# One transformer layer on one core: windowed attention whose contexts come out turned the other way, with a shorter selection and new orders of work

## The reference, cut to what matters

```python
h = concat([tokens(x), txt], axis=1)                 # (16, 165, 256): 1 + 36 + 128 tokens
h = h + attn(layernorm(h))
h = h + ffn(layernorm(h))                            # quantised matmuls, depthwise conv, silu

def attn(x):                                         # 16 query heads, 4 key heads, head size 16
    xq, xk = rope(x @ Wq), rope(x @ Wk)
    xv = x @ Wv
    keys, values = repeat(xk, 4), repeat(xv, 4)
    scores = einsum('bqhd,bkhd->bhqk', xq, keys) / 4
    mask = abs(idx[:, None] - idx[None, :]) <= 32    # a band of 65 keys
    attn = softmax(where(mask, scores, -inf))
    ctx = einsum('bhqk,bkhd->bqhd', attn, values).reshape(b, s, 256)
    return ctx @ Wo
```

## Time and profile before

| | |
|---|---|
| median of 3 runs | 399.84 us |
| the runs | 399.84, 400.05, 396.22 us |
| the profiled execution | 396.99 us |
| its span, first to last instruction | 395.2 us |
| mean granted TensorE clock | 0.987 of 2.4 GHz |
| PE busy | 364.5 us, 92% of the span |
| DVE, ACT, POOL busy | 301.8, 256.5, 215.0 us |

### The profile page before, as it was taken

How to read it: one execution, slowest core, us unless ns; L and a number is a source line. 1 busy time by engine, 2 the same in 40 slices (tenths; PEclk the granted TensorE clock), 3 DMA queues, 4 the chain that set the end, 5 groups by cost and what they waited for, 6 DMA issues and landing times.

```text
span 395.2 us, 8402 instructions
## 1 busy us (share of the span) xinstructions
PE 364.5 (92%) x3033; PEld 273.6 (69%) x3037; DVE 301.8 (76%) x639; ACT 256.5 (65%) x483; POOL 215.0 (54%) x245
## 2 busy tenths in 40 slices
PE   6799799999999999999989999999999988987886
PEld 2376557777877886678767876788678866853743
DVE  2246649654599879888998698959895998799795
ACT  3213436568786779677868686769767966672552
POOL 5406589688479928892689427971994006001000
PEclk9889989999999999999999999999999999999999
DMA  7671521201000012002000220022011100000101
GB/s 235 166 181 41 153 99 29 54 13 28 20 19 2 2 48 50 22 21 53 19 0 2 57 48 2 2 61 44 11 27 44 27 2 13 25 2 0 35 2 35
DMA packets 21907, 16.71 MB, mean 42 GB/s; under 512 B 12435, under 2 KB 20936, under 8 KB 21865
## 3 DMA queue, kind: packets, MB, share of 16 engines
q1 hardware_dynamic: 20970, 15.11, 15.3%
q10 hardware_dynamic: 895, 1.06, 1.0%
HBM read 9.82 MB, written 3.38 MB: 33 GB/s over the span
## 4 chain that ended last, share of the span: by engine, by line
PE 65%; DVE 17%; ACT 7%; issue 5%; DMA 4%; POOL 1%; SPq 1%; DVEq 0%; ACTq 0%; POOLq 0%
PE bank L1784 8%; PE bank L1864 8%; PE bank L1835 7%; PE bank L1878 6%; PE bank L1937 5%; PE bank L1938 4%; PE bank L1907 4%; DMA shared<-in_x 4%; PE bank L1855 3%; PE bank L1731 3%; PE bank L1981 3%; DVE shared L1635 2%; PE bank L1898 2%; PE bank L1797 2%; PE bank L1847 2%
## 5 line engine op out<-in xcount | busy, mean ns | idle before, releaser
L1501 DVE TENSOR_REDUCE mx<-bank 120x4 fp32r<-120x376 f32 (+3 forms) x88 | 44.1, 506 | 26.8 <-PE bank L1847 26.2
L1273 ACT COPY pT<-bank 94x480 f32<-94x480 f32 (+3 forms) x88 | 48.1, 554 | 21.7 <-PE bank L1864 21.3
L1265 ACT ACTIVATE pr<-bank 120x376 f32<-120x376 f32 (+3 forms) x88 | 39.6, 453 | 27.1 <-PE bank L1855 26.2
L1864 PE MATMUL bank<-cst,pr 120*94 120x120 f32 (+3 forms) x352 | 51.3, 270 | 2.6 <-ACT pr L1265 2.5
L1835 PE MATMUL bank<-kbd,q_hl 128*120 128x376 f32 (+3 forms) x176 | 51.1, 374 | 1.6 <-issue 0.9
L1113 POOL TENSOR_TENSOR rs<-ve,half_neg 110x3 f32<-110x3 f32 x16 | 16.7, 1044 | 62.8 <-DVE ve L1529 47.2
L1937 PE MATMUL bank<-xT_hi,w1T 128*128 128x330 f32 x128 | 44.2, 351 | 1.3 <-DVE late L1584 0.9
L1864 PEld LDWEIGHTS bank<-cst,pr 120*94 120x94 f32 (+3 forms) x352 | 36.1, 122 | 10.0 <-ACT pr L1265 6.0
L1120 POOL TENSOR_SCALAR xn<-h,mv,rs 110x256 f32<-110x256 f32 x21 | 27.6, 1321 | 25.3 <-PE bank L1772 24.9
L1135 POOL TENSOR_TENSOR rc<-qk,cst 110x320 f32<-110x320 f32 x22 | 20.0, 908 | 38.9 <-ACT qk L1236 37.9
L1938 PE MATMUL bank<-xT_lo,w1T 128*128 128x330 f32 x128 | 39.5, 314 | 0.0
(11 more groups left out here) (131 smaller groups left out, 877.7 us busy)
## 6 DMA issues: line engine op xcount, KB each, us to landing
kbd<-shared SPq DMA_DIRECT2D x56, 41.2 KB, 2.1
out<-h SPq DMA_DIRECT2D x7, 330.0 KB
wn<-in_w SPq DMA_DIRECT2D x2, 1024.0 KB, 6.6
shared<-in_x SPq DMA_DIRECT2D x4, 432.0 KB
h<-in_txt SPq DMA_DIRECT2D x1, 770.0 KB
late<-in_lin SPq DMA_DIRECT2D x1, 768.0 KB, 7.6
vw<-v_rows SPq DMA_DIRECT2D x8, 94.0 KB
v_rows<-qk SPq DMA_DIRECT2D x8, 82.5 KB
```

The source lines that it names most:

```text
L1265: nc.scalar.activation(pr[:, g % 3, 0:HKV * WIDTH[j]], S_BANKS[g % 2][0:QP, 0:HKV * WIDTH[j]], ACT.Exp, scale=HD ** -0.5).then_inc(exped, 1)
L1273: nc.scalar.copy(pT[0:WIDTH[j], g % 3, :], S_BANKS[g % 2][0:WIDTH[j], 0:HKV * QP]).then_inc(p_kept, 1)
L1501: nc.vector.tensor_reduce(mx[:, g % 4, :].bitcast(F32R), S_BANKS[g % 2][0:QP, 0:HKV * WIDTH[j]].rearrange("p (k c) -> p k c", k=HKV), axis ...
L1864: o = nc.tensor.transpose(S_BANKS[g % 2][0:w, kv * QP:(kv + 1) * QP], pr[:, g % 3, kv * w:(kv + 1) * w], ident[0:QP, 0:QP])
```

## The change: what it does

The operands of `context` change places. `pT` (the turned probabilities, 120 columns) is now the stationary operand and `vw` the moving one, cut to 17 columns (16 values and the ones; `VS` goes from 32 to 17). All four `kv` use the whole array instead of a strip each, and the result has queries on the partitions. So `keep_ctx` and `turn_ctx` are gone, `norm` reads `C_BANK` itself, and the bank is free for the next group when `norm` is done rather than when the copy is. `select` is one fp32 transpose for every two windows (48 in all), after which the two windows of a transpose lie in the lower and upper half of the partitions; `keep_sel` puts heads and windows in place with four copies of 64 partitions instead of one. The clearing of `vw` on POOL is left out. The four `keep_clock` products that stood behind the last `turn_ctx` stand behind the last `context`. All orders of work (the tables) are new.

```diff
-VS = 2 * HD
+VS = HD + 1
...
-                nc.scalar.copy(ctxP[:, :, js[0] * QB:(js[-1] + 1) * QB],
-                               N_BANK[:, 0:len(js) * QP // 2].rearrange("p (q c) -> p c q", c=2)).then_inc(sel_kept, 1)
+                at = js[0] * QB
+                turned = N_BANK[:, 0:(len(js) + 1) // 2 * QP].rearrange("p (i q c e) -> p e c i q", q=QB, c=2, e=2)
+                for odd in range(2):
+                    cnt = (len(js) + 1 - odd) // 2
+                    for e in range(2):
+                        dst = ctxP[QK * e:QK * (e + 1), :, at:at + len(js) * QB].rearrange("p c (j q) -> p c j q", q=QB)
+                        o = nc.scalar.copy(dst[:, :, odd::2, :], turned[QK * odd:QK * (odd + 1), e, :, 0:cnt, :])
+                o.then_inc(sel_kept, 1)
...
             def norm(n, k):
                 cnt = len(GROUPS[k])
-                dve.wait_ge(ctx_turned, NG * n + k + 1)
-                src = N_BANK[0:QP, 0:cnt * 128].rearrange("p (c v) -> p c v", v=VS)
+                dve.wait_ge(ctx_done, NB * n + GROUPS[k][-1] + 1)
+                if n or k:
+                    dve.wait_ge(ctx_picked, NG * n + k)
+                src = C_BANK[0:QP, 0:cnt * HKV * VS].rearrange("p (c v) -> p c v", v=VS)
...
                 if j % SLOTS == 0 and (n or k):
-                    pe.wait_ge(ctx_kept, NG * n + k)
-                col = (j % SLOTS) * QP
+                    pe.wait_ge(ctx_normed, NG * n + k)
                 for kv in range(HKV):
-                    o = nc.tensor.matmul(C_BANK[VS * kv:VS * (kv + 1), col:col + QP], vw[n % 2][0:WIDTH[j], j, :, kv],
-                                         pT[0:WIDTH[j], g % 3, kv * QP:(kv + 1) * QP], start=True, stop=True)
+                    at = (j % SLOTS * HKV + kv) * VS
+                    o = nc.tensor.matmul(C_BANK[0:QP, at:at + VS], pT[0:WIDTH[j], g % 3, kv * QP:(kv + 1) * QP],
+                                         vw[n % 2][0:WIDTH[j], j, :, kv], start=True, stop=True)
                 o.then_inc(ctx_done, 1)
...
             def select(n, k):
...
-                half = QP // 2
-                for c in range(len(GROUPS[k])):
-                    for e in range(2):
-                        o = nc.tensor.matmul(N_BANK[QK * e:QK * (e + 1), c * half:(c + 1) * half], ctxn[:, c, :],
-                                             ident[0:QP, e:QP:2], start=True, stop=True)
+                cnt = len(GROUPS[k])
+                for c in range(0, cnt, 2):
+                    src = ctxn[:, c:min(c + 2, cnt), :].rearrange("p c v -> p (c v)")
+                    o = nc.tensor.transpose(N_BANK[0:QK * min(2, cnt - c), c // 2 * QP:(c // 2 + 1) * QP], src,
+                                            ident[0:QP, 0:QP])
                 o.then_inc(ctx_picked, 1)
...
 ONCE = {
-    'pe.patches': (3, 4, 11, 12),
+    'pe.patches': (2, 10, 11, 17),
```

More of the change, by code:

```diff
@@ L143 @@
     'pe.turn_xn': (
[L144 to L151, removed]
+        (3, 4),
+        (18, 21),
+        (67, 70),
+        (129, 139),
+        (208, 213),
+        (284, 290),
+        (356, 361),
+        (428, 433),
     ),
     'pe.project': (
[L154 to L159, removed]
@@ L160 @@
-        (383, 388, 399),
-        (461, 464, 475),
+        (6, 7, 9),
+        (26, 29, 36),
+        (76, 78, 97),
+        (151, 154, 167),
+        (223, 231, 241),
+        (298, 303, 308),
+        (365, 371, 379),
+        (448, 451, 456),
     ),
     'pe.turn_q': (
[L164 to L171, removed]
+        (12, 13, 15),
@@ L172 @@
+        (45, 50, 59),
+        (101, 111, 120),
+        (178, 186, 194),
+        (247, 256, 268),
+        (318, 335, 340),
+        (386, 391, 403),
+        (474, 477, 489),
     ),
     'pe.turn_k': (
[L174 to L181, removed]
+        (14, 16),
+        (62, 65),
+        (123, 126),
+        (200, 204),
+        (273, 277),
+        (343, 346),
+        (406, 417),
@@ L242 @@
+        (112, 147, 160),
+        (182, 209, 234),
+        (259, 283, 309),
+        (332, 376, 385),
+        (411, 432, 457),
+        (479, 509, 526),
+        (546, 569, 584),
     ),
     'pe.out_proj': (
[L244 to L251, removed]
+        (55, 85, 92),
+        (116, 155, 164),
+        (188, 217, 238),
+        (270, 306, 312),
@@ L252 @@
+        (342, 382, 389),
+        (420, 454, 460),
+        (496, 522, 529),
+        (557, 581, 585),
     ),
     'pe.turn_xs': (
[L254 to L261, removed]
+        (128,),
+        (199,),
+        (272,),
+        (347,),
+        (421,),
+        (493,),
+        (560,),
+        (590,),
     ),
     'pe.up': (
[8 rows of a table removed]
[8 rows of a table added]
     ),
     'pe.turn_max': (
-        (176,),
-        (253,),
-        (329,),
@@ L277 @@
[L277 to L281, removed]
+        (173,),
+        (246,),
+        (319,),
+        (395,),
+        (468,),
+        (538,),
+        (586,),
+        (600,),
     ),
     'pe.spread': (
[L284 to L291, removed]
+        (179,),
+        (249,),
+        (323,),
+        (400,),
+        (472,),
+        (542,),
+        (587,),
@@ L292 @@
+        (601,),
     ),
     'pe.down': (
[L294 to L301, removed]
+        (189, 191, 195),
+        (262, 263, 266),
+        (336, 337, 338),
+        (412, 413, 414),
+        (483, 484, 488),
+        (551, 552, 555),
+        (588, 589, 591),
+        (602, 602, 602),
     ),
     'dve.stats1': (
-        (5,),
@@ L305 @@
-        (9,),
+        (4,),
+        (10,),
         (13,),
-        (17,),
+        (18,),
         (37,),
-        (101,),
-        (149,),
+        (97,),
+        (146,),
         (198,),
@@ L343 @@
     'dve.max_s': (
[8 rows of a table removed]
[8 rows of a table added]
     ),
     'dve.norm': (
[L354 to L361, removed]
+        (23, 30, 40),
+        (48, 56, 67),
+        (91, 104, 127),
+        (142, 154, 175),
+        (190, 203, 227),
+        (238, 251, 272),
+        (285, 306, 321),
+        (334, 346, 366),
     ),
     'dve.add_att': (
[L364 to L371, removed]
+        (31, 41, 44),
+        (53, 79, 84),
+        (98, 126, 134),
+        (150, 178, 183),
+        (199, 228, 233),
+        (247, 275, 280),
+        (298, 322, 328),
+        (344, 367, 370),
     ),
@@ L532 @@
+        (123, 131, 133),
+        (172, 179, 184),
+        (225, 231, 233),
+        (270, 273, 278),
+        (326, 336, 337),
     ),
     'act.keep_k': (
-        (16, None),
-        (46, 49),
-        (89, 93),
-        (144, 148),
-        (198, 201),
-        (250, 257),
-        (307, 311),
-        (358, 362),
+        (17, None),
+        (45, 47),
+        (85, 86),
+        (137, 139),
+        (188, 189),
+        (236, 239),
+        (284, 288),
+        (339, 346),
     ),
     'act.exp': (
[8 rows of a table removed]
[8 rows of a table added]
@@ L582 @@
+        (77, 102, 114),
+        (126, 147, 165),
+        (182, 204, 217),
+        (232, 264, 269),
+        (285, 310, 319),
+        (333, 359, 365),
+        (378, 389, 402),
     ),
     'act.quant_x': (
-        (83,),
-        (135,),
-        (188,),
-        (243,),
-        (297,),
-        (351,),
-        (401,),
+        (78,),
+        (129,),
+        (180,),
+        (230,),
+        (283,),
+        (332,),
+        (377,),
         (),
@@ L716 @@
         (10,),
-        (12,),
-        (16,),
+        (13,),
+        (15,),
         (19,),
-        (22,),
+        (20,),
         (25,),
@@ L1349, in _ @@
             work = {name: due("act." + name) for name in (
-                "exp", "keep_xn", "keep_qk", "keep_q", "keep_ctx", "keep_sel", "quant_x", "high_x", "mid", "keep_p", "keep_k", "tanh", "abs_g", "conv_g", "keep_w", "sort_a", "keep_pix_a", "keep_patch")}
+                "exp", "keep_xn", "keep_qk", "keep_q", "keep_sel", "quant_x", "high_x", "mid", "keep_p", "keep_k", "tanh", "abs_g", "conv_g", "keep_w", "sort_a", "keep_pix_a", "keep_patch")}
             for q in TICKS:
@@ L1359, in _ @@
                     keep_q(n, t)
-                for n, k in work["keep_ctx"].get(q, ()):
-                    keep_ctx(n, k)
                 for n, k in work["keep_sel"].get(q, ()):
@@ L1985, in _ @@
             work = {name: due("pe." + name) for name in (
-                "shift", "context", "scores", "turn_p", "turn_xn", "project", "turn_q", "turn_k", "turn_ctx", "select", "out_proj", "turn_xs", "up", "turn_max", "spread", "down", "turn_pix", "patches", "sum_w", "turn_w")}
+                "shift", "context", "scores", "turn_p", "turn_xn", "project", "turn_q", "turn_k", "select", "out_proj", "turn_xs", "up", "turn_max", "spread", "down", "turn_pix", "patches", "sum_w", "turn_w")}
             for q in TICKS:
@@ L2003, in _ @@
                     turn_k(n, part)
-                for n, k in work["turn_ctx"].get(q, ()):
-                    turn_ctx(n, k)
                 for n, k in work["select"].get(q, ()):
```

322 lines of the change are left out of this document (134 added, 188 removed), and 176 rows, old and new, of the table ORDER.

## The result

| | before | changed |
|---|---|---|
| median | 398.5 us (396.22 to 400.05, 4 runs) | 409.56 us (408.43 to 410.15, 4 runs) |
| ratio, 95% interval | | 1.0286 (1.0236 to 1.0335) |
| profiled execution, span | 396.99, 395.2 | 409.78, 408.0 |
| mean granted clock of it | 0.987 | 0.979 |

The change costs 11.1 us by the medians (12.8 between the spans of the two profiled executions; that of before lies 1.5 us under its median). I had forecast 403.

The account below looks back on a forecast made before the run. The prediction took PE to bound the kernel in the middle, from 60 to 340 us. PE's sum +8.9, start -1 and waits -3 made +4.9 us on 396.99, so 401.9, or 403 on a median; range 391 to 412.

Parts of the forecast that it names:

- PE bounds the middle, a us for a us, as long as the waits do not move: From 60 to 340 us, each us added to or taken from PE's stream changes the time by about a us.
- PE's sum, +8.9 us (5.4 to 13.8): PE's stream: new contexts 72.9 us plus selection 4.9, less 68.9 removed; the ends come from the load's cost.
- The waits give back 3 us: In the middle, a third of PE's 9.9 us of idle time closes under the new orders: -3 us.
- The start, -1 us: First pair's projection: one block of tokens leaves its way and covers a PE wait; -1 us, between 0 and 2.9.
- The selection's copies: keep_sel on ACT: four copies of about 0.26 or 0.21 us, net ACT +3.3 us, no bound by itself.
- DVE and the bank: nothing: A group's first context waits for norm instead of a copy: about nothing, up to 0.3 us a group if late.
- The sum of the forecast: Whole kernel: +4.9 us on the profiled 396.99 gives 401.9; with runs on average 1.7 above, 403 on a median.
- Columns decide: Rival: context instructions cost by moving columns, loads pulled ahead; PE loses 47 us, time 370 to 380; chance 0.06.
- Waits fall, loads are cheap: Rival: load at its low end, nearly all middle waits close, start gains 2.9; 391.5, or 394 on a median; chance 0.16.
- the change does nothing: Rival: the load costs as said and the orders give all of it back; 397 to 402; chance 0.16.
- Waits take the place: Rival: keep_sel's copies and norm hold PE 0.3 us per group (+7), or load at upper end; 409 to 413; chance 0.20.

Follow-up runs that it names:

- experiment 4: Kernel before with one more full-array fp32 product of 17 columns (two instructions) per context: 410.81 us, ratio 1.0285.
- 9: Changed kernel with three of the four key heads' context products, a quarter of the contexts left out: 401.47 us, ratio 1.0072.
- experiment 8: Kernel before with the new selection's transposes and keep_sel as one copy, the order of the heads left out: 396.41 us, ratio 0.9964.
- 6: Changed kernel with both operands of the context products in fp32r instead of fp32, 18 value columns: 401.42 us, ratio 0.9985.
- Experiment 1: Changed kernel with 32 moving value columns per context instruction instead of 17: 409.33 us, ratio 1.023.
- experiment 11: Changed kernel again, unaltered, in six runs beside the kernel before on one chip: 410.51 us, ratio 1.0307.
- 7: Changed kernel with keep_sel as one copy instead of four, the order of the heads left out: 410.35 us, ratio 1.0236.
- Experiment 2: Changed kernel with the order tables of the kernel before, removed steps dropped: 462.44 us, ratio 1.1476.
- 5: Changed kernel with each context product loading 60 of its 120 stationary columns, half of the queries' contexts left out: 402.28 us, ratio 1.0057.

## Why the prediction was wrong, point by point

**PE bounds the middle, a us for a us, as long as the waits do not move.** Upward this did not fail by much: between the two profiles PE is busy 17.2 us more and idle 4.4 less, 3.1 of it in the middle, which makes the 12.8 us of span. By the medians and ratios a us added is worth 0.65 to 0.7 (experiment 4; 0.84 between profiles), and the prediction's own 8.9 less 3 for waits is 0.66 per us. Downward it failed: 0.5 to 0.6 from the changed kernel (9), 0.4 or less from before (8, where 4.7 us gave 1.9 by the medians and no span between the profiles), and with 37 us taken away (6) at most 14 come back, as POOL and DVE come up. Few waits in a list do not make an engine the only bound; the others were close behind.

**PE's sum, +8.9 us (5.4 to 13.8).** This is the step that failed, a term mis-sized: the page shows +17.2, beyond the upper end. Its mechanism was right, and the instruction costs 0.105 as taken. By the matmul records without waits, contexts, turns and selection by themselves add 21.4 us (19.6 in the sum), but all other work of PE gives back only 4.2, where the sum had 10.7 for the drains that go, less the loads that come out behind contexts. So the miss lies mainly in what the change does to the work around it, and in the clock.

The same piece by piece: I worked the pieces out from all matmul records in order, by how much each moves the end of the work before it. The contexts add 72.4 us (72.9 forecast), but the load that each run of them exposes behind it is another 6.1 in the middle, where the 72.9 had contained both: some 5.6 too little. The selection adds 6.1 where 4.9 stood, and 1.2 behind it. On the other side more went than I had said: contexts 31.9 + 11.7 behind them (42.0 forecast), turn_ctx 12.1 with its waits (9.7), selection 15.9 with its waits + 3.5 (17.2), so 75.1 for 68.9. That makes 85.8 - 75.1 = 10.7, not far from 8.9, but with some 3 us of waits among what went.

Experiment 1, whose middle kept nearly all of its clock, has 13.6 of busy time; the other three us behind 10.7 are those waits, which are no busy time, and loads exposed in other places of the new order (behind mask products and turn_q, +2.6), less what fell elsewhere. The rest, 3.6 of 17.2, goes with the half clock: it is the difference between two profiles with one and with three such stretches in the middle, not a cost measured by itself.

**The granted clock** stood nowhere in the forecast. It costs some 2.5 to 3.3 us, sure to 2 (experiment 11). Nothing in the trace of before announced it: its middle was at 1.00.

**The waits give back 3 us.** Right: from 9.9 to 6.8 in the middle. Experiment 4 shows the same 3.3 with the old orders, so added work fills the waits without any new orders.

**The start, -1 us.** Wrong: 0.1. The wait of 1.77 us is gone, but the block of image tokens now stands at 42.40, ahead of the first scores, and takes its 2.77 us there.

**The selection's copies.** Their size was right (0.26 and 0.21 forecast, 0.252 and 0.205 measured; ACT +3.7, forecast +3.3), and so was it that they would not bound the changed kernel. That they are nearly harmless only under orders made for them, I had not said: 5.4 to 6.7 us in experiment 8 against some 2 to 3 in 7.

**DVE and the bank: nothing.** Right under the new orders, where norm holds no context in the list. Experiment 2 shows what it is worth otherwise.

**The sum of the forecast.** 401.9 and 1.7 make 403.6 and not 403; it changes nothing.

**The rivals.** "Columns decide" falls by experiment 1. "Waits fall, loads are cheap" and "the change does nothing" fall by the time. "Waits take the place" named the right time, 409 to 413, with the wrong mechanism: PE waits for the copies for 0.6 us in all, and the load was not at its upper end. That it named the right time is luck. What decided is PE's own work, larger by half than my sum before the clock and nearly twice it with the clock, at two thirds of a us per us: 17.2 x 0.65 = 11.2, and 11.1 was measured. That product takes its rate from experiment 4 and isn't an independent proof (with 0.84, the rate between profiles, it is 14.4, for 12.8 of span), but 9, in the other direction, agrees roughly. What stays open is why the clock falls where it does, and how the gap between 8.7 to 9.5 us at full clock and the 13.6 of busy time divides between waits filled and other engines.

No version here beats the kernel before clearly: experiment 8 is 0.4% faster but leaves out the order of the heads, and 6 is equal to it with contexts in fp32r.

## What to carry to other kernels

Turning a product so that its long operand is stationary trades moving columns for a load per instruction; in fp32 here that load is paid twice, since a product is two instructions. Count load times instructions first, then the load exposed behind each run, and only then the copies that fall away. Before calling an engine the bound, add a little work to it and see how much of it comes out in the time.

## What was not expected of the hardware

- The granted clock fell to half with PE busy for 3.1 to 3.2 of the 3.4 us ahead and for all of the stretch, at the same places in two profiles (217.7 and 217.0; 323.6 and 322.8 us), and out_proj took 2.04 us there instead of 1.03. With lighter loads on PE (5, 6) the clock was lower on average, not higher: in one run it stood at 0.75 for most of the time, 0.743 on average, and that run took 442.81 us against 397.54 of the fastest.
- An fp32 product with 17 moving and 120 stationary columns costs 2 x 0.105 us, one in fp32r 0.105; with 60 stationary columns most instructions start 0.055 us apart, 0.067 on average, at a clock of 0.74. The load sets the pace in both types, and 15 more moving columns change it by nothing that shows (0.77 to 0.78 us for eight against 0.75).
- Leaving the strips of the array cost 0.18 us ahead of an fp32 product, some 12 us in all behind the 75 runs of contexts, and it went when the strips went; about half of it came back as exposed loads.
